# Layer 1's first attention turned round: P streamed past stationary features, denominators from a row of ones

## The chip, the core and the metric

The kernel runs on one core of one Trainium2 chip. The metric is the device time of one execution in microseconds, the median of several runs. Engines are named as in the profile: PE (matrix products), PEld (its weight loads), DVE (vector), ACT (activation), POOL, SP (issues the transfers).

## What is computed

Four graph-attention layers are applied to `x`, 32 batches of 512 nodes by 256 features, each after a layer norm and a relu. The change touches only the first of the two attentions in layer 1, where every node attends to every node (no mask), with 512 features:

```python
def _gat(inp, adj_mask, W, a):
    h = jnp.matmul(inp, W)
    f1 = jnp.matmul(h, a[:F_, 0])
    f2 = jnp.matmul(h, a[F_:, 0])
    e = jax.nn.leaky_relu(f1[:, :, None] + f2[:, None, :], ALPHA)
    ...
    att = jax.nn.softmax(e, axis=2)
    h_prime = jnp.einsum('bij,bjf->bif', att, h)
    return jax.nn.elu(h_prime)
out = jax.nn.relu(jnp.matmul(x, mlp1_w) + mlp1_b)
residual = out
out = _gat(jax.nn.relu(out), None, W_fc, a_fc)
out = jax.nn.elu(out) + residual
out = jax.nn.relu(jnp.matmul(out, mlp2_w) + mlp2_b)
```

Then comes a second attention under the mask, and layers 2 and 3. The elu is applied twice: for a negative y the result is exp(exp(y)-1)-1.

## The kernel before

Everything stays on the core. Batches run in three lanes (`s = b % 3`) with buffers of their own; each lane has a ring of PSUM banks, three for lanes 0 and 1, two for lane 2, and every use of a bank waits until its last reader is done (`freed`). Each engine has a generator per batch, cut into steps by `yield`; the strings in `TURNS` say, digit by digit, which batch's generator runs its next step on that engine. The order of every engine is thus fixed in the program, and in the steady state one cycle of it does one batch's worth of work, taken from up to six batches at once. Waits are on semaphores named for what is produced (`at("Plo", b, j)`).

Exact float32 products are made from three products of rounded parts (`mm3`, L516: hi by hi, hi by lo, lo by hi). ACT copies the high part out of a bank (`...hi`), DVE subtracts to get the low part (`...lo`).

In layer 1 of a batch: `turn` transposes the normalized input, `m1` is the first matrix, its relu stands in `O1` (features on the partitions, also the residual), its parts in `oT`. `project` (bank `h1`) gives features 256 to 511 and the scores, into `HA`; bank `hs2` gives features 0 to 255, into `HB`, which is the lane's `hT`. `HA` carries a column of ones. The exponentials P (source nodes on the partitions, 512 targets along the row) go to `R`, and their parts to `oT`, which is free by then (`Phi`, `Plo`). The attention itself is `attf`: for each block of 128 targets the block of P is the stationary operand and the features move past it, 258 columns of `HA` and 256 of `HB`; the ones give the denominator in column 256. So nodes lie on the partitions; ACT scales by the reciprocal (L1145, L1147) and the elu is done on 256 columns at a time by ACT and DVE (L878, L884, L1136). Since `m2` wants features on the partitions, 16 transposes (`zT`, L658) turn the result, and DVE adds it to `O1` (L902). `top` (L552) and `row` (L562) spread a maximum and a row of scores over the partitions, `attend` (L574) and the loop at L607 are the other attentions, `weigh` (L779) makes their P.

Of the kernel before, what the change touches and what calls it, by code (L numbers as in the profile page):

```python
# [34 lines left out]
    "Phi": (4,), "Plo": (4,), "attf": (8,), "rDf": (4,),  # L35
# [16 lines left out]
    + [("attf", q, "ef", (q, 1)) for q in range(8)] + [("zT", k, "o2", (k,)) for k in range(4)]  # L52
# [29 lines left out]
    "dve": (
        ("wwwwwwwww0000ww0000000000000ww000w000w0000w00ww0w0w0w000001w10000w00110w1110000101011100100000000010"
         "111000000w000101000100001100100000000111111000111111010100000010001000000022000101110212002112112210"
         "2202120010201211201121101120100001020111111221211212010110112111111111211221200210112200002212122011"
         "110000000"),
        ("2122222221122202022111212201100001110221000020120012202211110211211222112201210201101010111111112211"
         "12111111111101000022201110022220010100211122122222"),
        ("5455555555445535345454545534355344334343453535453545444454435453445345545435443534434443433443554544"
         "3444443344443444435355444335553534343535344455455545443444444342444343243344233234432232223424223443"  # L90
         "4423333324333332422434422442343343323332233223334324433333233333332342434332244242422332442334334443"
         "4433333223331332123323323322112332221131131231332132222113222223233123132313221213121222221113222322"
         "3122222222222211113313222131331311212311322223333233221222221222201210212122100122111120000201002211"
         "2211021121111202120200012201112000011111011211102211110110100210111111202101120200220012102221111211"
         "0011111111110111020101001102002011011011000001001010111010100010000000000111000000001000001001001111"
         "000000001000000000000001000001100000100000100000000000001010000000"),
    ),
# [66 lines left out]
def build(nc, x_d, adj_d, L0_W, L0_a, m1_w, m1_b, m2_w, m2_b, fc_w, fc_a, ha_w, ha_a, L2_W, L2_a, L3_W, L3_a, out_d):  # L164
    ctx = ExitStack()
    with ctx:
# [571 lines left out]
        def vector_batch(e, w, b):  # L738
# [151 lines left out]
            for q in range(8):  # L890
# [4 lines left out]
                if q > 1:  # L895
                    yield from joined(q - 2)
# [433 lines left out]
```

## Time and profile before

| | us |
|---|---|
| median of three runs (3109.88 to 3122.49) | 3118.48 |
| time of the profiled execution | 3117.49 |
| its span, first to last instruction | 3115.7 |
| PE busy | 3039.2 |
| DVE busy | 2453.6 |
| ACT busy | 2326.1 |

The span is the time between the first and the last instruction in the trace; 1.8 us of the execution lie around it. Busy time counts each moment once for an engine. A PE busy time is no measure of what PE could do, since the end of each product is modelled and overlaps the next; the distance between two starts is the better price.

### The profile page before, as it was taken

The page shows a single profiled execution, that of the slowest core. Times are in us where ns is not written, and L with a number is a line of the kernel's source. Part 1 is how long each engine was busy: PE and PEld are TensorE (multiplying, and loading weights), DVE is VectorE, ACT ScalarE, POOL GpSimd, SP SyncE. Part 2 cuts the span into 40 slices and gives each one's busy share as a digit, 9 for nine tenths or more (in the row PEclk, how much of TensorE's full clock was granted, in tenths as well). Part 3 has the DMA queues.
Part 4 walks back from the last instruction along what each step waited for, and adds up shares of the span by engine and source line. Part 5 has one row for each costly group of instructions (what it writes and reads, how often), then busy time and mean ns, then how long its engine had stood idle before and what let it go on. Part 6 is the DMA issues. An engine that isn't in the chain of part 4 may idle for free.

```text
span 3115.7 us, 58739 instructions
## 1 busy us (share of the span) xinstructions
PE 3039.2 (98%) x21504; PEld 2843.7 (91%) x21504; DVE 2453.6 (79%) x7049; ACT 2326.1 (75%) x6303; POOL 202.2 (6%) x410
## 2 busy tenths in 40 slices
PE   7999999999999999999999999999999999999996
PEld 7899999999999999999999999999999999999985
DVE  5787887887887888877888878878878878878764
ACT  6678777777778777778777778777777787787674
POOL 2000000000000000000000000000000000000000
PEclk8999999999999999999999999999999999999997
DMA  2000000000000000000000000000000000000000
GB/s 75 1 8 15 15 15 15 15 1 15 15 15 15 15 1 15 15 15 15 15 1 15 15 15 15 8 7 15 15 15 15 2 14 15 15 15 8 1 8 14
DMA packets 16335, 41.54 MB, mean 13 GB/s; under 512 B 5296, under 2 KB 6832, under 8 KB 16048
## 3 DMA queue, kind: packets, MB, share of 16 engines
q1 hardware_dynamic: 16048, 37.77, 3.4%
q8 instruction: 173, 2.83, 0.4%
q14 instruction: 114, 0.93, 0.1%
HBM read 20.99 MB, written 16.78 MB: 12 GB/s over the span
## 4 chain that ended last, share of the span: by engine, by line
PE 85%; ACT 8%; DVE 6%; issue 1%; SPq 0%; POOL 0%; DMA 0%; DVEq 0%; POOLq 0%; ACTq 0%
PE bank L516 46%; PE bank L574 15%; PE bank L607 14%; ACT Z L1031 4%; PE bank L562 3%; PE bank L530 2%; PE bank L658 2%; DVE R L779 2%; PE bank L552 1%; DVE x L996 1%; DVE Z L993 1%; ACT Z L1183 1%; ACT Z L1189 1%; ACT Z L1178 0%; PE bank L684 0%
## 5 line engine op out<-in xcount | busy, mean ns | idle before, releaser
L574 PE MATMUL bank<-hw,R 128*128 128x257 f32 x3072 | 713.1, 385 | 4.0 <-ACT hw L1069 3.0
L574 PEld LDWEIGHTS bank<-hw,R 128*128 128x128 f32 x3072 | 572.9, 192 | 79.5 <-issue 4.6
L607 PEld LDWEIGHTS bank<-hw,R 128*128 128x128 f32 x4096 | 496.4, 193 | 8.3 <-issue 3.8
L607 PE MATMUL bank<-hw,R 128*128 128x65 f32 x4096 | 499.6, 271 | 3.6 <-DVE R L779 3.6
L779 DVE SCALAR_TENSOR_TENSOR R<-bank,E,mask_ne 128x512 f32<-128x512 f32 x640 | 450.3, 742 | 14.7 <-PE bank L562 12.9
L1031 ACT ACTIVATE Z<-x,nm,rs 128x256 f32<-128x256 f32 x512 | 283.4, 593 | 55.9 <-DVE x L996 34.1
L1234 POOL TENSOR_TENSOR rs<-ve,mhalf 128x4 f32<-128x4 f32 x128 | 134.6, 1052 | 2858.7 <-DVE ve L731 2141.3
L516 PE MATMUL bank<-wfc_hi,oThi 128*128 128x256 f32 (+1 forms) x1024 | 302.8, 296 | 1.9 <-DVE oTlo L858 1.9
L516 PE MATMUL bank<-wfc_lo,oThi 128*128 128x256 f32 (+1 forms) x1024 | 290.5, 284 | 0.0
L516 PE MATMUL bank<-wfc_hi,oTlo 128*128 128x256 f32 (+1 forms) x1024 | 290.5, 284 | 0.0
L1054 ACT COPY Z<-bank 128x258 f32<-128x258 f32 (+1 forms) x512 | 183.5, 370 | 100.9 <-PE bank L516 100.4
L516 PEld LDWEIGHTS bank<-wfc_hi,oThi 128*128 128x128 f32 x1024 | 194.7, 190 | 3.7 <-DVE oTlo L858 2.6
L516 PEld LDWEIGHTS bank<-wfc_hi,oTlo 128*128 128x128 f32 x1024 | 195.2, 191 | 0.0
L516 PEld LDWEIGHTS bank<-wfc_lo,oThi 128*128 128x128 f32 x1024 | 195.0, 190 | 0.1
L1069 ACT ACTIVATE hw<-Z,hw 128x256 f32<-128x256 f32 x384 | 180.0, 502 | 1.2
L562 PE MATMUL bank<-identr,E 128*128 128x128 f32 x1024 | 154.2, 275 | 8.2 <-ACT E L1063 8.2
L516 PE MATMUL bank<-HAhi,oThi 128*128 128x258 f32 x512 | 161.0, 314 | 0.3 <-DVE oTlo L872 0.3
L1145 ACT ACTIVATE Z<-bank,rD 128x256 f32<-128x256 f32 x256 | 123.1, 481 | 45.2 <-DVE rD L893 37.9
L530 PE MATMUL bank<-identr,Z 128*128 128x128 f32 x1024 | 139.8, 280 | 10.3 <-ACT Z L1031 10.0
L516 PE MATMUL bank<-HAlo,oThi 128*128 128x258 f32 x512 | 145.4, 284 | 0.0
L516 PE MATMUL bank<-HAhi,oTlo 128*128 128x258 f32 x512 | 145.1, 283 | 0.0
L1008 ACT ACTIVATE Z<-x,sx 128x256 f32<-128x256 f32 x256 | 128.5, 505 | 20.2 <-DVE x L970 20.1
(260 smaller groups left out, 8306.1 us busy)
## 6 DMA issues: line engine op xcount, KB each, us to landing
x<-in_x_dram SPq DMA_DIRECT2D x32, 512.0 KB, 3.4
out_dram<-x SPq DMA_DIRECT2D x32, 512.0 KB, 2.6
R<-in_adj_dram SPq DMA_DIRECT2D x2, 512.0 KB, 5.9
Z<-in_L_gnn_mlp_w_dram SPq DMA_DIRECT2D x2, 512.0 KB, 5.4
O<-in_L_gnn_W_fc_dram SPq DMA_DIRECT2D x1, 1024.0 KB, 6.9
R<-in_L_gnn_W_dram SPq DMA_DIRECT2D x1, 256.0 KB, 3.7
R<-in_L_gnn_W_hand_dram SPq DMA_DIRECT2D x1, 256.0 KB, 6.7
rowt<-in_L_gnn_W_dram SPq DMA_DIRECT2D x1, 256.0 KB, 4.7
```

The costliest lines, as they stand in the source:

```text
L516: i = e.matmul(out, u, v, start=first and q == 0, stop=last and q == 2, skip_group_check=not group)
L530: i = e.transpose(bk[:, n * 128:(n + 1) * 128], hn[:, n, k * 128:(k + 1) * 128], ident[:, :])
L562: i = e.transpose(bk[:, n * 128:(n + 1) * 128], m["E"][:, 0, h, n:n + 1].broadcast_to([128, 128]), ident[:, :])
L574: ins = e.matmul(bk[:, 0:257], P[:, j, i * 128:(i + 1) * 128], hw[:, j, 0:257], start=(j == 0), stop=(j == NBLK - 1))
L607: ins = e.matmul(bk[:, i * 66:i * 66 + 65], P[:, (4 * h + j) % PTILES, i * 128:(i + 1) * 128], hv[:, j, h, 0:65], start=(j == 0 and i == 0 ...
L779: e.scalar_tensor_tensor(P[:, t, :], bank_of(b, "row", p)[:, :], m["E"][:, 1, h, j:j + 1], mask[:, j, :], ALU.max, ALU.mult).then_inc(up(" ...
L1008: e.activation(hns[b % LANES][:, n, :] if l else junk[:, n, :], xs[b % XSLOTS][:, n, :], ACT.Square, bias=m["sx"][:, n:n + 1], scale=-floa ...
L1031: e.activation(hn[:, n, :], x[:, n, :], ACT.Relu, bias=m["nm"][:, n:n + 1], scale=m["rs"][:, n:n + 1]).then_inc(up("hn", b))
L1054: e.copy(raw[s][:, i, 0:n], bank_of(b, f"h{l}", i)[:, 0:n]).then_inc(up("raw", b))
L1069: e.activation(hw[:, n, 0:256], raw[s][:, n, 0:256], ACT.Copy, scale=hw[:, n, 256:257]).then_inc(up("hw", b))
L1145: e.activation(Z[s][:, q * 256:(q + 1) * 256], bank_of(b, "attf", q)[:, 0:256], ACT.Relu, scale=rd).then_inc(up("ef", b))
L1234: e.tensor_tensor(m["rs"][:, :], m["ve"][:, :], mhalf[:, :], ALU.pow).then_inc(up("rs", b))
```

## The change

The roles in `attf` are exchanged. 128 features of `HA` or `HB` are now stationary (`FO` is the order of the four blocks), and the 512 columns of P move past them, so results have features on the partitions, 512 nodes along the row. The denominators come from eight products of their own (`dn`) with a stationary block of ones, which put them on all partitions of one bank. DVE takes the reciprocal of that bank, 512 wide, multiplies each result by it, adds the positive part to `O1` and cuts the negative part (`value`); ACT does two exponentials, DVE the last addition (`joined`). The transposes and their additions are gone. The parts of the sum are kept in `HA` and `hT` instead of `oT`. `m2` takes its blocks in the order of `FO`. `TURNS` is written anew for all engines.

```diff
 ONCE = {
...
-    "Phi": (4,), "Plo": (4,), "attf": (8,), "rDf": (4,),
-    "ef": (8, 2), "mf": (8,), "ef2": (8,), "zf": (8,), "zT": (4,), "o2": (4,), "o2hi": (4,), "o2lo": (4,),
+    "Phi": (4,), "Plo": (4,), "dn": (1,), "rDf": (1,), "attf": (4,), "yf": (4, 3), "ef": (4, 2), "o2": (4,),
+    "o2hi": (4,), "o2lo": (4,),
...
-    + [("attf", q, "ef", (q, 1)) for q in range(8)] + [("zT", k, "o2", (k,)) for k in range(4)]
+    + [("dn", 0, "rDf", (0,))] + [("attf", t, "yf", (t, 0)) for t in range(4)]
...
 TURNS = {
     "pe": (
-        ("wwww00w00000w000000w000ww0ww00ww000ww0w0w0w001www1w1w100w0000110100010000100121111000000000000100111"
+        ("wwwww00ww0000w0000000ww0000011w0w00000ww0001w11w1ww1w00w11000011000w01101000w001111w0w01000010011w100"
...
-        HA = {p: sb(f"HA{p}", [128, NBLK, F + 2], F32R) for p in PARTS2}
+        HA = {p: sb(f"HA{p}", [128, NBLK, F], F32R) for p in PARTS2}
+        FO = (2, 3, 0, 1)
+        ones = sb("ones", [128, 2], F32R)
+        HA2 = {p: HA[p].rearrange("p (k h) n -> p k (h n)", h=2) for p in PARTS2}
+        hwf = [hws[s].rearrange("p b n -> p (b n)") for s in range(LANES)]
+        rden = [hwf[s][:, 512:1024] for s in range(LANES)]
+        yfb = [[R[s][:, 4, :], rowt[s][:, :], hwf[s][:, 0:512]] for s in range(LANES)]
...
-            for q in range(8):
-                i, H, n = q // 2, (HA, HB[s])[q % 2], 258 - q % 2 * 2
-                cols = slice(i * 128, (i + 1) * 128)
-                w.wait_ge(*freed(b, "attf", q))
+            w.wait_ge(*freed(b, "dn", 0))
+            w.wait_ge(s_id, 1)
+            for j in range(NBLK):
+                w.wait_ge(*at("Plo", b, j))
+                for p in PARTS2:
+                    i = e.matmul(bank_of(b, "dn", 0)[:, :], ones[:, 0:1].broadcast_to([128, 128]), oT[p][:, j, :],
+                                 start=j == 0 and p == "hi", stop=j == NBLK - 1 and p == "lo")
...
+            for t, fo in enumerate(FO):
+                H, c0 = (HB[s], HA)[fo // 2], fo % 2 * 128
+                w.wait_ge(*freed(b, "attf", t))
                 for j in range(NBLK):
-                    w.wait_ge(*at("Plo", b, j))
-                    w.wait_ge(*at(("hAlo", "hBlo")[q % 2], b, j))
-                    ins = mm3(e, bank_of(b, "attf", q)[:, 0:n], (oT["hi"][:, j, cols], oT["lo"][:, j, cols]),
-                              (H["hi"][:, j, 0:n], H["lo"][:, j, 0:n]), j == 0, j == NBLK - 1)
...
+                    w.wait_ge(*at(("hBlo", "hAlo")[fo // 2], b, j))
+                    ins = mm3(e, bank_of(b, "attf", t)[:, :], (H["hi"][:, j, c0:c0 + 128], H["lo"][:, j, c0:c0 + 128]),
+                              (oT["hi"][:, j, :], oT["lo"][:, j, :]), j == 0, j == NBLK - 1)
...
-            for fo in range(4):
-                w.wait_ge(*freed(b, "zT", fo))
...
-                    i = e.transpose(bk[:, n * 128:(n + 1) * 128], Z[s][:, n * 512 + c0:n * 512 + c0 + 128], ident[:, :])
...
+                            tuple((HA2, hT[s])[t // 2][p][:, t % 2, :] for p in PARTS2), t == 0, t == 3)
...
+            def value(t, fo):
+                y = yfb[s][t % 3]
+                w.wait_ge(*at("attf", b, t))
+                e.tensor_tensor(y, bank_of(b, "attf", t)[:, :], rden[s], ALU.mult).then_inc(up("yf", b))
+                w.wait_ge(*at("yf", b, t, 0))
+                e.scalar_tensor_tensor(O1[:, fo, :], y, 0.0, O1[:, fo, :], ALU.max, ALU.add).then_inc(up("yf", b))
+                e.tensor_scalar(y, y, 0.0, None, ALU.min).then_inc(up("yf", b))
+                yield
+
+            def joined(t, fo):
+                w.wait_ge(*at("ef", b, t, 1))
+                w.wait_ge(*at("yf", b, t, 1))
+                e.scalar_tensor_tensor(O1[:, fo, :], yfb[s][t % 3], -1.0, O1[:, fo, :], ALU.add, ALU.add).then_inc(up("o2", b))
+                yield
...
+            w.wait_ge(*at("dn", b, 0))
+            e.reciprocal(rden[s], bank_of(b, "dn", 0)[:, :]).then_inc(up("rDf", b))
...
+            for t, fo in enumerate(FO):
+                yield from value(t, fo)
+                if t > 0:
+                    yield from joined(t - 1, FO[t - 1])
+                if t > 1:
+                    yield from low_o2(t - 2, FO[t - 2])
...
-                w.wait_ge(*at("m2", b - 1, 1))
+                w.wait_ge(*at("attf", b - 1, 3))
                 w.wait_ge(*at("o2lo", b - 1, 3))
...
+            for t in range(4):
+                y = yfb[s][t % 3]
+                w.wait_ge(*at("yf", b, t, 2))
+                e.activation(y, y, ACT.Exp).then_inc(up("ef", b))
+                yield
+                w.wait_ge(*at("ef", b, t, 0))
+                e.activation(y, y, ACT.Exp, bias=minus1[:, 0:1]).then_inc(up("ef", b))
```

What moves on the engines is shown at three places of the steady state. Names are those of the buffers: `hw2,R2` is the attention of lane 2, `tm0` the maximum of lane 0, `Z` holds normalized input or projected features. First PE after the projection of layer 1's second attention (`wha`), before the change:

```order
L516 MATMUL bank0<-wha_hi,hT0lo 128x258
L574 MATMUL bank7<-hw2,R2 128x257 [waits P_2,hw_2,sc_2]
L552 MATMUL bank1<-identr,tm0 128x128 [waits sc_0,raw_0]
L574 MATMUL bank7<-hw2,R2 128x257 [waits P_2,hw_2] x3
L562 MATMUL bank2<-identr,E0 128x128 [waits E_0,raw_0]
L562 MATMUL bank2<-identr,E0 128x128 x3
L574 MATMUL bank6<-hw2,R2 128x257 x4
L574 MATMUL bank7<-hw2,R2 128x257 [waits y3_2]
```

PE at the same place with the change:

```order
L520 MATMUL bank2<-wha_hi,hT0lo 128x258
L578 MATMUL bank6<-hw2,R2 128x257 [waits P_2,hw_2] x3
L556 MATMUL bank0<-identr,tm0 128x128 [waits sc_0,raw_0]
L578 MATMUL bank7<-hw2,R2 128x257 x4
L566 MATMUL bank1<-identr,E0 128x128 [waits E_0,raw_0]
L566 MATMUL bank1<-identr,E0 128x128 x3
L578 MATMUL bank6<-hw2,R2 128x257 [waits y3_2]
L578 MATMUL bank6<-hw2,R2 128x257 x3
```

Three products of lane 2 instead of one stand ahead of the transpose of `tm0`.

Second PE between the transposes for `m1` and `m1` itself, before the change:

```order
L530 MATMUL bank3<-identr,Z1 128x128 [waits hn_1] x4
L530 MATMUL bank4<-identr,Z1 128x128 [waits y0]
L530 MATMUL bank4<-identr,Z1 128x128 x3
L530 MATMUL bank7<-identr,Z2 128x128 [waits hn_2,y3_2]
L530 MATMUL bank7<-identr,Z2 128x128 [waits hn_2] x3
L530 MATMUL bank6<-identr,Z2 128x128 [waits y3_2]
L530 MATMUL bank6<-identr,Z2 128x128 x3
L516 MATMUL bank5<-hT1hi,wm1_hi 128x512 [waits hTlo_1,y0]
L516 MATMUL bank5<-hT1lo,wm1_hi 128x512
```

PE at the same place with the change:

```order
L534 MATMUL bank3<-identr,Z1 128x128 [waits hn_1] x4
L534 MATMUL bank4<-identr,Z1 128x128 [waits y0]
L534 MATMUL bank4<-identr,Z1 128x128 x3
L520 MATMUL bank6<-w0_hi,hT2hi 128x264 [waits raw_2]
L520 MATMUL bank6<-w0_lo,hT2hi 128x264
L520 MATMUL bank6<-w0_hi,hT2lo 128x264
L520 MATMUL bank6<-w0_hi,hT2hi 128x264
L520 MATMUL bank6<-w0_lo,hT2hi 128x264
L520 MATMUL bank6<-w0_hi,hT2lo 128x264
L520 MATMUL bank7<-w0_hi,hT2hi 128x264 [waits raw_2]
L520 MATMUL bank7<-w0_lo,hT2hi 128x264
L520 MATMUL bank7<-w0_hi,hT2lo 128x264
```

The transposes of lane 2 stood between; now four steps of `w0` products do, of which the last three rows are not shown; after them comes `m1`.

Third DVE. Before the change, from the first `attf` of a batch on:

```order
L893 RECIPROCAL rD0<-bank1 128x1 [waits attf]
L968 SCALAR_TENSOR_TENSOR Z2<-Z2 128x256 [waits e2]
L970 SCALAR_TENSOR_TENSOR x0,sx2<-Z2,x0 128x256 [waits x2]
L878 TENSOR_SCALAR R0<-R0 128x256 [waits ef]
L779 SCALAR_TENSOR_TENSOR R1<-bank4,E1,mask_ne 128x512 [waits row_1]
L731 TENSOR_SCALAR ve2<-sq2 128x4 [waits sq_2]
L779 SCALAR_TENSOR_TENSOR R1<-bank4,E1,mask_ne 128x512 [waits att0]
L878 TENSOR_SCALAR R0<-R0 128x256 [waits ef]
L893 RECIPROCAL rD0<-bank0 128x1 [waits attf]
L779 SCALAR_TENSOR_TENSOR R1<-bank4,E1,mask_ne 128x512 [waits att0]
L884 SCALAR_TENSOR_TENSOR Z0<-R0,Z0 128x256 [waits ef2]
L779 SCALAR_TENSOR_TENSOR R1<-bank4,E1,mask_ne 128x512 [waits att0]
```

The products that wait on these rows are `attf` of lane 0. DVE with the change, from the variance of lane 2 (`ve2`) on:

```order
L732 TENSOR_SCALAR ve2<-sq2 128x4 [waits sq_2]
L899 RECIPROCAL hw0<-bank1 128x512 [waits dn]
L780 SCALAR_TENSOR_TENSOR R1<-bank4,E1,mask_ne 128x512 [waits att0,rDf]
L780 SCALAR_TENSOR_TENSOR R1<-bank4,E1,mask_ne 128x512 [waits att0]
L879 TENSOR_TENSOR R0<-bank2,hw0 128x512 [waits attf]
L881 SCALAR_TENSOR_TENSOR O1<-R0,O1 128x512 [waits yf]
L882 TENSOR_SCALAR R0<-R0 128x512
L780 SCALAR_TENSOR_TENSOR R1<-bank4,E1,mask_ne 128x512 [waits att0]
L879 TENSOR_TENSOR rowt0<-bank0,hw0 128x512 [waits attf]
L881 SCALAR_TENSOR_TENSOR O1<-rowt0,O1 128x512 [waits yf]
L882 TENSOR_SCALAR rowt0<-rowt0 128x512
```

The next rows of DVE there:

```order
L888 SCALAR_TENSOR_TENSOR O1<-R0,O1 128x512 [waits ef]
L879 TENSOR_TENSOR hw0<-bank1,hw0 128x512 [waits attf]
L881 SCALAR_TENSOR_TENSOR O1<-hw0,O1 128x512 [waits yf]
L882 TENSOR_SCALAR hw0<-hw0 128x512
L747 TENSOR_TENSOR hT2lo<-bank7,hT2hi 128x512 [waits hThi_2]
L747 TENSOR_TENSOR hT2lo<-bank6,hT2hi 128x512 [waits hThi_2]
L793 CAST hsr2<-hs2 128x2
L795 TENSOR_TENSOR hsr2<-hs2,hsr2 128x2 [waits hs_2]
```

The reciprocal of 512 columns stands behind the variance `ve2` and ahead of two blocks of P of lane 1 (`R1`), and the low parts `hT2lo` and the sums `hsr2` of lane 2 stand behind three whole `value` steps.

## Rows read from the trace of the kernel before

**Rows 1.** The page: its head and section 1.

```profile
span 3115.7 us, 58739 instructions
...
PE 3039.2 (98%) x21504; PEld 2843.7 (91%) x21504; DVE 2453.6 (79%) x7049; ACT 2326.1 (75%) x6303; POOL 202.2 (6%) x410
```

**Rows 2.** Windows, 400 to 2800: busy us (count) of PE, PEld, DVE, ACT, POOL; clock.

```profile
400.00:2800.00 2400.00, 2379.73 (x17008) 2231.24 (x17007) 1936.72 (x5594) 1838.33 (x5003) 149.46 (x309) 1.00 0.04 13
```

**Rows 3.** Chain of waits in order of time: start, us, what.

```profile
1520.90 0.87 PE bank L658 x8
...
1531.20 0.84 PE bank L607 x8
...
1536.98 2.73 DVE R L779 x4
...
1543.48 5.22 PE bank L574 x24
...
1630.82 2.73 DVE R L779 x4
```

**Rows 4.** Timeline of PE, 1514 to 1531: start, us, instruction.

```profile
1515.67 0.28 PE L516 MATMUL bank<-hT0hi,oThi 128*128 128x256 f32 x1
...
1517.09 0.60 PE L562 MATMUL bank<-identr,E 128*128 128x128 f32 x4
...
1525.79 0.40 PE L516 MATMUL bank<-oTlo,wm_hi 128*128 128x512 f32 x1
...
1530.81 0.39 PE L516 MATMUL bank<-oThi,wm_lo 128*128 128x512 f32 x1
```

**Rows 5.** Groups by form, DVE and ACT: busy us, mean ns of one, idle before.

```profile
L902 DVE TENSOR_TENSOR O<-bank,O 128x512 f32<-128x512 f32 x128 | 85.3, 686 | 59.0 <-PE bank L658 59.0
...
L867 DVE TENSOR_SCALAR R<-rowt,E 128x512 f32<-128x512 f32 x128 | 63.4, 536 | 0.0
...
L884 DVE SCALAR_TENSOR_TENSOR Z<-rowt,Z 128x256 f32<-128x256 f32 x128 | 54.1, 424 | 13.9 <-ACT rowt L1136 6.8
...
L878 DVE TENSOR_SCALAR R<-R 128x256 f32<-128x256 f32 x128 | 37.3, 293 | 40.9 <-ACT R L1147 40.9
...
L1145 ACT ACTIVATE Z<-bank,rD 128x256 f32<-128x256 f32 x256 | 123.1, 481 | 45.2 <-DVE rD L893 37.9 <-PE bank L516 3.0 <-issue 0.6
...
L1136 ACT ACTIVATE R<-R,minus 128x256 f32<-128x256 f32 x128 | 67.1, 524 | 0.2 <-DVE R L878 0.2
...
L1147 ACT ACTIVATE rowt<-bank,rD 128x256 f32<-128x256 f32 x128 | 63.0, 492 | 0.0
...
L1090 ACT ACTIVATE Z<-Z 128x256 f32<-128x256 f32 x128 | 53.4, 417 | 4.1
```

**Rows 6.** The three lines with RECIPROCAL: ns min/median/max of one.

```profile
L788 DVE RECIPROCAL rD<-D x384: 162/164/166, 138.0 to 3110.7; 128x1 f32<-128x1 f32 x192
...
L834 DVE RECIPROCAL rD<-D x128: 177/178/180, 34.7 to 2947.6; 128x4 f32<-128x4 f32 x128
...
L893 DVE RECIPROCAL rD<-bank x128: 154/168/170, 97.2 to 3015.6; 128x1 f32<-128x1 f32 x128
```

**Rows 7.** Timeline at 1555 to 1558, PE and DVE, ahead of `m1`.

```profile
1555.46 2.02 PE L530 MATMUL bank<-identr,Z 128*128 128x128 f32 x16
1557.92 0.47 PE L516 MATMUL bank<-hT1hi,wm_hi 128*128 128x512 f32 x1 [0.44 <-DVE hT1lo L746]
...
1557.09 1.29 DVE L746 TENSOR_TENSOR hT1lo<-bank,hT1hi 128x512 fp32r<-128x512 f32 x2 [0.25 <-ACT hT1hi L1048]
```

**Rows 8.** Timeline of PE at 1540 to 1542, ahead of layer 1's maximum.

```profile
1540.44 0.60 PE L574 MATMUL bank<-hw,R 128*128 128x257 f32 x2
1541.36 0.29 PE L552 MATMUL bank<-identr,tm 128*128 128x128 f32 x1 [0.33 <-DVE tm L753]
```

**Rows 9.** Timeline, 1502 to 1507: end of layer 2's attention, then its variance.

```profile
1502.29 0.47 PE L516 MATMUL bank<-HAhi,oThi 128*128 128x258 f32 x1
...
1506.81 0.17 DVE L731 TENSOR_SCALAR ve<-sq 128x4 f32<-128x4 f32 x1
```

More of the change, by code:

```diff
@@ L885, in joined @@
                 yield
-            def exf(q):
-                return (R[s][:, 4, 0:256], R[s][:, 4, 256:512], rowt[s][:, 0:256], rowt[s][:, 256:512])[q % 4]
-            for q in range(8):
-                if q % 2 == 0:
-                    w.wait_ge(*at("attf", b, q))
-                    e.reciprocal(m["rD"][:, 0, q // 2:q // 2 + 1], bank_of(b, "attf", q)[:, 256:257]).then_inc(up("rDf", b))
-                    yield
-                if q > 1:
-                    yield from joined(q - 2)
-                yield from small(q)
@@ L898, in vector_batch @@
-            yield from joined(6)
-            yield from joined(7)
-            for k in range(4):
-                w.wait_ge(*at("zT", b, k))
-                e.tensor_tensor(O1[:, k, :], bank_of(b, "zT", k)[:, :], O1[:, k, :], ALU.add).then_inc(up("o2", b))
-                yield
-                if k:
-                    w.wait_ge(*at("o2hi", b, k - 1))
-                    e.tensor_tensor(oT["lo"][:, k - 1, :], O1[:, k - 1, :], f32(oT["hi"][:, k - 1, :]),
-                                    ALU.subtract).then_inc(up("o2lo", b))
-                    yield
@@ L1129, in scalar_batch, with parts @@
                 yield
[L1131 to L1154 removed]
+            def parts(t):
+                w.wait_ge(*at("o2", b, t))
+                w.wait_ge(*at("attf", b, t // 2 * 2 + 1))
+                e.copy((HA2, hT[s])[t // 2]["hi"][:, t % 2, :], O1[:, FO[t], :]).then_inc(up("o2hi", b))
+                yield
+            for t in range(4):
+                y = yfb[s][t % 3]
+                w.wait_ge(*at("yf", b, t, 2))
+                e.activation(y, y, ACT.Exp).then_inc(up("ef", b))
+                yield
+                w.wait_ge(*at("ef", b, t, 0))
+                e.activation(y, y, ACT.Exp, bias=minus1[:, 0:1]).then_inc(up("ef", b))
                 yield
+                if t:
+                    yield from parts(t - 1)
+            yield from parts(3)
             for fo in range(2):
@@ L1284, in _ @@
             w.wait_ge(s_const, 1)
-            for p, q, v in (("hi", F, -2.0), ("hi", F + 1, 0.0), ("lo", F, 0.0), ("lo", F + 1, 0.0)):
-                e.tensor_scalar(HA[p][:, :, q], mhalf[:, :], v, None, ALU.mult)
+            e.tensor_scalar(ones[:, :], mhalf[:, 0:2], -2.0, None, ALU.mult)
             e.tensor_copy(identr[:, :], id_st).then_inc(s_id)
```

140 lines of the change are left out of this document (56 added, 84 removed).

## The prediction

> **What bounds the kernel now.** I read the page's busy times first. PE is busy for 98% of the span, DVE for 79%, ACT for 75% [rows 1]. In the steady stretch PE is busy for 2379.7 of 2400 us at full clock, DVE for 1936.7, 81% [rows 2]. So the end of every batch's work is set by PE, and another engine costs something only where PE waits for it. The chain of waits in order of time gives the length of a cycle: the same piece, four blocks of P by L779, comes at 1536.98 and again at 1630.82, 93.84 us later [rows 3]. Some 28 of the 32 batches pass in this manner; the rest is ramp and tail.
>
> PE's busy time is modelled, so I price its products by the distance of starts. Twelve products of 256 columns take from 1515.67 to 1517.09, 0.118 each; 22 steps of 512 columns take from 1525.79 to 1530.81, 0.228 each [rows 4]. A transpose is 0.87/8 = 0.109, a 65-column product 0.84/8 = 0.105 (0.21 for one in the program, which issues two), a 257-column one 5.22/24 = 0.2175 (0.435 in the program) [rows 3].
>
> Where does PE wait in the cycle? Two places. Ahead of `m1`, 16 transposes begin at 1555.46 and are issued by 1555.46 + 16 x 0.109 = 1557.20, but the first product starts at 1557.92, after DVE's low part began at 1557.09: 0.7 us lost [rows 7]. Ahead of `tm0`, two halves of a 257-column product from 1540.44 end at 1540.88, the transpose starts at 1541.36: 0.5 us lost [rows 8]. With small waits behind both I take 1.5 us of old waits in a cycle.
>
> **PE's own work.** Removed per batch: 96 products of 256 or 258 columns, 96 x 0.118 = 11.33, and 16 transposes, 1.74, together 13.07 us. Added: 8 + 48 = 56 products of 512 columns, 56 x 0.228 = 12.77. Saved: 0.30 a batch, 10 us in all. The columns are nearly equal; what is saved is half the starts. Unknown is whether the products with a broadcast block of ones cost the same: between 0.118 (the cheaper product, -0.9 a batch) and 0.24 I take 0.228, since the engine streams the same 512 columns.
>
> **The old waits.** The new order puts three 257-column products of lane 2 ahead of `tm0` where one stood: 2 x 0.435 = 0.87 more cover against 0.5 lost [rows 3, 8]. Between the second half of the transposes and `m1` stand twelve `w0` products, 12 x 0.118 = 1.4, where eight transposes stood, 0.87: 0.55 more against 0.7 lost [rows 3, 4, 7]. Both waits go nearly or wholly: -1.5.
>
> **ACT.** Removed: 8 relus (L1145, 0.481), 8 exponentials (L1147, 0.49), 8 with a bias (L1136, 0.52): 11.9 us [rows 5]. Added: four of each exponential at 512 columns. No exponential of 512 columns is in the rows; the 256 more cost between nothing and DVE's step for as many, 0.686 - 0.42 = 0.27, and I take 0.21, nearer to the latter since the engine streams too: 0.417 + 0.21 = 0.63 (L1090) and 0.73, together 5.5. ACT loses 6.4 us a batch. It is not the bound, so this is worth nothing by itself.
>
> **DVE.** Removed: 8 x 0.29 (L878), 8 x 0.42 (L884), 4 x 0.686 (L902), 4 x 0.168 (L893): 9.1 us [rows 5, 6]. Added four times: the multiplication from the bank 0.69 (as L902), the positive part 0.69, the cut 0.54 (as L867), the joining 0.69: 10.4 us, 1.95 of it in one `value` step. Then one reciprocal of 512 columns, which no row shows. Bounds: if it streamed like L902, 0.69. By L788 and L834, one column takes 164 ns and four take 178, so 4.7 ns a column: 164 + 511 x 4.7 = 2.55 us. By the farthest pair (154 of L893, 180 of L834), 8.7 ns a column: 4.6 us [rows 6]. I take 2.55, because the medians are of the same operand and spread by 2 ns. DVE's load then rises from 1936.7/2400 x 93.84 = 75.7 us a cycle [rows 2, 3] by 3.9 to 79.6 of some 92: it is still not the bound, but its order becomes tight.
>
> The page "VectorE: DVE Perf Modes" of the Trainium skill, section "First, the fixed hardware budget", says that the reciprocal is an iterative divide with a repeat count of 8. If that meant eight cycles a column at the 0.96 GHz it gives, one would take about 4.4 us (an estimate from the page), and the sum below would be 1.9 us a cycle higher. The step of 4.7 ns in the rows is nearer to half of that.
>
> **The new wait.** It is in DVE's order after `dn`. Put zero where PE has issued the last `dn`. PE's list from there: two `attf` of 12 x 0.228 = 2.74 (done 5.5), 1.3 us of lane 1, the third `attf` (6.8 to 9.5), eight transposes of lane 2, the fourth (10.4 to 13.2), then the small products `hsr2`, which need DVE's `hT2lo` and `hsr2`. DVE: `ve2` closes layer 2's norm. Before, the next product after that attention starts at 1502.29 and `ve` at 1506.81, 4.5 us [rows 9]; part of this is DVE's other work, so I take 3.6, and the attention now ends 1.8 before zero. The reciprocal behind `ve2` thus runs from 1.8 to 4.35; two blocks of P at 2.73/4 = 0.68 [rows 3] to 5.7; `value` to 7.7; P to 8.4; `value` to 10.3; the joining to 11.0; `value` to 13.0; two `hT2lo` (0.69) to 14.4; `hsr2` to about 14.8. PE wants it at 13.2: a new wait of 1.6 us. Behind it are queued, on PE, lane 2's last projection and `m2` of lane 0, so the whole cycle moves. Going on likewise, the third low part of the sum, behind three more joinings and a `value`, reaches `m2` some 0.4 to 0.5 late; I take 0.2 more for other places with less cover than before. New waits: 2.3, none of which I can see in a row; the bounds are 0.3 (a short reciprocal, the third `value` then waits only for its product) and 4.3 (the long one).
>
> **Sum.** Per cycle -0.30 - 1.5 + 2.3 = +0.5, and over 28 cycles +14, less the saving on the four other batches, 1: from the profiled 3117.5 to about 3130. The old waits' remainder could be larger than 1.5 and my walk ignores that DVE catches up; I put the median 5 us lower, 3125. The profiled execution is within 1 us of the median of the runs, so no shift is needed.
>
> **Rivals.**
> Fast: the reciprocal takes about 1 us or less, or DVE reaches it earlier. Then the wait ahead of `hsr2` is at most 0.3 and `m2`'s is gone; -0.30 - 1.5 + 0.5 = -1.3, 28 times: 3080, at best 3065. For it: all three old waits lose their cause and bank rings are used five times instead of twelve. Against: the 4.7 ns step.
>
> Slow: the reciprocal takes 3.5 to 4.6 us. It stands on the DVE path to `hsr2`, so each us above 2.55 is a us of PE, from the point where DVE is already late (about 1 us, by the walk). 0.95 to 2.05 more, 28 times: 3157 to 3187. For it: the farthest pair of rows. Against: the medians. The rule of that page of the Trainium skill would give about 4.4 us and so 3170, by the same walk.
>
> No effect: 512-column products at 0.236 and no reciprocal wait but the old ones elsewhere: 3118. It falls into the same band as my forecast.
>
> DVE as the bound: at 79.6 + 2 it would need 10 us more a cycle; I give it nothing of its own.
>
> **Chances.** The forecast (reciprocal near 2.6, waits exchanged, 3100 to 3150) 0.45; fast 0.30; slow 0.25. A difference of about 0.5%, 15.6 us, is what a measurement of this kernel can tell from none. Of the first case I put 0.34 within it, 0.04 below, 0.07 above; of the fast case nearly all is below, of the slow one nearly all above. Faster 0.33, same 0.36, slower 0.31. The range takes in the fast case from 3065 and the slow one to 3175; the forecast's own range is 3100 to 3150.
>
> **What the profile will show.** Right: PE's products of 512 columns 0.23 apart and 19,700 instructions instead of 21,504; RECIPROCAL 128x512 near 2.6 us; no idle ahead of `tm0` and `m1`; PE idle ahead of the first product on `hsr`, put down to DVE; DVE at about 85% in the steady stretch, ACT at 70%. Wrong: the reciprocal off by over 1 us either way; or PE waiting ahead of something that I did not list, such as layer 1's projection behind the last `m1`, or the transposes of layer 0.

## The result, and the profile after

The changed kernel takes 3189.5 us (median of 4 runs, 3185.6 to 3193.7) against 3114.2 us (3109.7 to 3122.5) for the kernel before on the same chip: ratio 1.024, 95% interval 1.021 to 1.027. The forecast was 3125, its range ended at 3175. The time is lost in the steady part. I take the length of a cycle from the start of the four transposes ahead of layer 0's maximum in one batch to the same in the next, mean over 22 cycles: 94.10 us before, 96.66 after, and 28 x 2.56 = 72 of the 75 us. Executions of one and the same kernel fall into two groups 8 to 16 us apart, with a higher and a lower mean granted clock (0.991 and 0.985 in the kernel before), so small differences are read from the cycle and not from the medians.

The page after, its head and busy times:

```profile
span 3183.8 us, 54320 instructions
...
PE 3065.3 (96%) x19712; PEld 2750.1 (86%) x19712; DVE 2607.4 (82%) x6822; ACT 2195.4 (69%) x5791; POOL 206.0 (6%) x410
```

The window from 400 to 2800 us of the same trace, columns as in [rows 2]:

```profile
400.00:2800.00 2400.00, 2341.25 (x15198) 2103.57 (x15197) 2006.07 (x5271) 1690.60 (x4479) 145.63 (x297) 1.00 0.03 12
```

PE lost 38 us of busy time in the window, DVE gained 69, ACT lost 148. The mean clock rounds to 1.00, as in [rows 2], but it is not full throughout. In the kernel before no stretch of this window is at the lower of the two levels; here four are, 3.4 us each, at 778, 1358, 1938 and 2518 us. One of them by the same view, and two products of 512 columns in it on PE's timeline, which start 0.43 us apart:

```profile
1357.85:1361.27 3.42, 3.40 (x10) 2.90 (x11) 2.29 (x4) 2.06 (x4) 0.00 (x0) 0.51 0.00 0
...
1359.63 0.63 PE L520 MATMUL bank<-oThi,hT1lo 128*128 128x512 f32 x1
1360.06 0.63 PE L520 MATMUL bank<-oThi,hT1hi 128*128 128x512 f32 x1
```

At full clock they are 0.23 apart. Each of the four stretches begins within 0.3 us of the end of a wait of 1.85 us, and the cycle that holds it lasts 98.3 us where the cycle at the same place of the three lanes' rotation lasts 96.8: 1.5 us more. So 6 of the 72 us are the clock's.

The groups of instructions, by form, give the prices that no row showed before:

```profile
L899 DVE RECIPROCAL hw<-bank 128x512 f32<-128x512 f32 x32 | 107.2, 3351 | 0.0
...
L881 DVE SCALAR_TENSOR_TENSOR O<-R,O 128x512 f32<-128x512 f32 x64 | 44.3, 692 | 2.2
...
L879 DVE TENSOR_TENSOR R<-bank,hw 128x512 f32<-128x512 f32 x64 | 43.7, 683 | 0.1
L882 DVE TENSOR_SCALAR R<-R 128x512 f32<-128x512 f32 x64 | 26.9, 420 | 0.0
```

The two exponentials on ACT, in the same view:

```profile
L1144 ACT ACTIVATE R<-R,minus 128x512 f32<-128x512 f32 x64 | 45.8, 715 | 0.9
L1141 ACT ACTIVATE R<-R 128x512 f32<-128x512 f32 x64 | 40.5, 633 | 127.4 <-DVE R L882 127.3
```

The reciprocal takes 3.35 us, not 2.55. The waits of PE over the whole execution (engine, what waited, for whom: us in all, times, the longest):

```profile
PE bank L534 <- ACT Z L1030: 16.8, 23, 8.4
PE bank L520 <- DVE hw L899: 16.4, 11, 1.7
PE bank L520 <- DVE oTlo L859: 16.0, 26, 0.6
PE bank L566 <- DVE R L780: 14.8, 8, 1.9
PE bank L520 <- DVE hsr L795: 9.2, 10, 1.9
```

The first line is ramp and tail: 0.9 of its 16.8 us fall between 400 and 2800 us. The old waits ahead of `m1` and `tm0` [rows 7, 8] are gone from this list. Four others stand in it: for the reciprocal itself, for the last low part ahead of layer 1's projection (L859), for a block of P that stood behind the reciprocal (L780), and the one that I had forecast, for `hsr`. The forecast wait, on PE's timeline at 1558 us:

```profile
1557.68 0.40 PE L520 MATMUL bank<-oThi,hT0lo 128*128 128x512 f32 x1
1558.96 0.38 PE L520 MATMUL bank<-w_hi,hsr 128*128 128x256 f32 x1 [0.88 <-DVE hsr L795]
```

DVE's timeline of the same stretch, from the reciprocal to what PE waits for:

```profile
1545.84 3.35 DVE L899 RECIPROCAL hw<-bank 128x512 f32<-128x512 f32 x1
...
1557.36 1.28 DVE L747 TENSOR_TENSOR hT2lo<-bank,hT2hi 128x512 fp32r<-128x512 f32 x2
...
1558.75 0.16 DVE L795 TENSOR_TENSOR hsr<-hs,hsr 128x2 fp32r<-128x2 f32 x1
```

One cycle earlier, on PE's timeline between the first and the second `attf`, a wait that I had not forecast:

```profile
1450.45 0.40 PE L520 MATMUL bank<-oThi,HAlo 128*128 128x512 f32 x1
1452.57 0.50 PE L520 MATMUL bank<-oThi,HAhi 128*128 128x512 f32 x1 [1.72 <-DVE hw L899]
```

And one cycle later, on PE's timeline, the other one, ahead of a row of transposes:

```profile
1648.84 0.54 PE L566 MATMUL bank<-identr,E 128*128 128x128 f32 x3 [1.85 <-DVE R L780]
```

The same wait three cycles earlier ends at 1357.87. DVE's timeline ahead of it:

```profile
1350.70 3.35 DVE L899 RECIPROCAL hw<-bank 128x512 f32<-128x512 f32 x1
1354.09 1.41 DVE L780 SCALAR_TENSOR_TENSOR R<-bank,E,mask_ne 128x512 f32<-128x512 f32 x2
1355.41 0.68 DVE L879 TENSOR_TENSOR R<-bank,hw 128x512 f32<-128x512 f32 x1
...
1357.07 0.75 DVE L780 SCALAR_TENSOR_TENSOR R<-bank,E,mask_ne 128x512 f32<-128x512 f32 x1
```

The transposes need a bank that is free when the fourth and last block of P has read it (`freed`). That block stands behind the reciprocal and the first `value` step; the two right behind the reciprocal are the second and the third, and nothing of PE waits for them here.

The wait at 1452.57 is one for a bank. Lane 2 has two banks; the first `attf` sits in one, `dn` in the other, and the second `attf` needs the bank that the reciprocal still reads (`rDf` frees it). Lanes 0 and 1 have three.

### The profile page after: what moved, and what is told of

It is laid out like the page before. It is cut to its first block, busy times and chain, and to the rows that moved or that the text cites. A ratio compares the mean times of both kernels' runs of the same rounds, so it can differ in the third digit from the quotient of the medians.

```text
span 3183.8 us, 54320 instructions
## 1 busy us (share of the span) xinstructions
PE 3065.3 (96%) x19712; PEld 2750.1 (86%) x19712; DVE 2607.4 (82%) x6822; ACT 2195.4 (69%) x5791; POOL 206.0 (6%) x410
## 4 chain that ended last, share of the span: by engine, by line
PE 62%; DVE 20%; ACT 16%; issue 1%; POOL 0%; SPq 0%; DMA 0%; POOLq 0%; DVEq 0%; ACTq 0%
PE bank L520 32%; PE bank L611 12%; PE bank L578 11%; DVE R L780 5%; ACT Z L1030 4%; DVE hw L899 3%; PE bank L566 2%; ACT oThi L1105 2%; ACT O L1103 2%; PE bank L534 2%; DVE Z L992 1%; DVE x L995 1%; ACT Z L1171 1%; PE bank L685 1%; ACT Z L1176 1%
## 5 line engine op out<-in xcount | busy, mean ns | idle before, releaser
L578 PE MATMUL bank<-hw,R 128*128 128x257 f32 x3072 | 725.9, 384 | 3.6 <-ACT hw L1068 1.0
L780 DVE SCALAR_TENSOR_TENSOR R<-bank,E,mask_ne 128x512 f32<-128x512 f32 x640 | 458.4, 744 | 30.2 <-PE bank L611 23.8
L534 PE MATMUL bank<-identr,Z 128*128 128x128 f32 x1024 | 146.2, 280 | 18.7 <-ACT Z L1030 16.8
L566 PEld LDWEIGHTS bank<-identr,E 128*128 128x128 f32 x1024 | 119.6, 143 | 42.5 <-issue 21.6
L534 PEld LDWEIGHTS bank<-identr,Z 128*128 128x128 f32 x1024 | 120.2, 143 | 37.2 <-ACT Z L1030 18.4
L1218 ACT ACTIVATE Z<-bank,rD 128x256 f32<-128x256 f32 x128 | 59.3, 465 | 131.7 <-DVE rD L789 131.5
L1141 ACT ACTIVATE R<-R 128x512 f32<-128x512 f32 x64 | 40.5, 633 | 127.4 <-DVE R L882 127.3
```

The costliest lines, as they stand in the source:

```text
L534: i = e.transpose(bk[:, n * 128:(n + 1) * 128], hn[:, n, k * 128:(k + 1) * 128], ident[:, :])
L566: i = e.transpose(bk[:, n * 128:(n + 1) * 128], m["E"][:, 0, h, n:n + 1].broadcast_to([128, 128]), ident[:, :])
L578: ins = e.matmul(bk[:, 0:257], P[:, j, i * 128:(i + 1) * 128], hw[:, j, 0:257], start=(j == 0), stop=(j == NBLK - 1))
L780: e.scalar_tensor_tensor(P[:, t, :], bank_of(b, "row", p)[:, :], m["E"][:, 1, h, j:j + 1], mask[:, j, :], ALU.max, ALU.mult).then_inc(up(" ...
```

## Experiments on the reciprocal

Theory A: the loss is the time that DVE spends on the reciprocal. The rivals were that the new order or the new waits cost by themselves. The first four kernels:

```diff
# e1_no_reciprocal, in the changed kernel (the quotient is a constant, the division is left out)
-            e.reciprocal(rden[s], bank_of(b, "dn", 0)[:, :]).then_inc(up("rDf", b))
+            e.tensor_scalar(rden[s], bank_of(b, "dn", 0)[:, :], 0.0, 2e-29, ALU.mult, ALU.add).then_inc(up("rDf", b))
# e2_reciprocal_twice: a second one, unused, into yfb[s][2]
# e3_half_reciprocal: 256 columns divided, the other 256 set to a constant (half the division left out)
# e4_before_with_reciprocal, in the kernel before, ahead of the first small reciprocal; its result is unused
+                        e.reciprocal(R[s][:, 4, :], P[:, 0, :])
```

> The kernel after with the 512-wide reciprocal replaced by one tensor_scalar of the same bank (times 0 plus a constant), about 0.65 us in place of 3.35; the division by the denominators is left out, all else stays. Theory A, the length of the reciprocal on DVE is what PE waits for at three places (the second attf product and the row of lane 2, the sums of layer 3): 1.6 to 2.7 us a cycle come back, 3189 falls to 3115 to 3145, and the waits on L899, R L780 and hsr go. Rival B, the new order itself is bad (projection right behind m1, fewer covers), whatever DVE does: less than 15 us come back, 3175 or more.

Measured: 3125.5 us (ratio to before 1.001, 0.999 to 1.003), cycle 94.76 us.

> The kernel after with the reciprocal on 256 columns and a constant on the other 256 (half of the division left out): DVE 1.1 to 1.3 us shorter there. A: a line between the others, 25 to 35 us less than 3189, near 3155 to 3165. B: no change, 3185.

Measured: 3140.6 us (1.007, 1.005 to 1.010), cycle 95.23 us: 14 us below A's range, so half the columns give back three quarters of the loss. Its reciprocal of 256 columns took 1746 ns:

```profile
L900 DVE RECIPROCAL hw<-bank 128x256 f32<-128x256 f32 x32 | 55.9, 1746 | 0.0
```

> The kernel after with a second, unused 512-wide reciprocal of the same bank ahead of the one that counts: 3.35 us more of DVE at that place. A: DVE is already late there, so nearly all of it shows, 2.8 to 3.35 us a cycle, 3270 to 3290. B: DVE's time is not what PE waits for, under 3215.

Measured: 3333.9 us (1.070, 1.066 to 1.073), cycle 101.14 us: 4.5 us a cycle for the second 3.35 us, more than any theory had.

> The kernel before with one additional 512-wide reciprocal (of a tile of P, result unused) on DVE ahead of its first small one: 3.35 us more of DVE at the same place of the program. A: it costs there too, since DVE is 81% busy and its work is queued behind: 1 to 2.7 us a cycle, 3145 to 3190. B: the order before absorbs it, under 3130.

Measured: 3192.7 us (1.025, 1.022 to 1.029), cycle 96.66 us, 3 us above A's range. The reciprocal took 3345 ns, here on a tile in SBUF. That the cycle equals the changed kernel's is chance: in every third cycle of this trace the clock is at its lower level for 3.4 us, in the changed kernel in every sixth.

So the reciprocal's length accounts for 64 of the 75 us, and the kernel before, with none of the new order, loses as much to it. The cost is not linear: cycles of 94.76, 95.23, 96.66 and 101.14 us for 0.7 us (the step in its place), 2.2 (1.75 and a 0.42 us step for the other half), 3.35 and 6.64 us on DVE. The first 2 us are nearly covered.

The last step, 4.5 us of cycle for 3.3 us of DVE, has the clock in it. Over the same 22 cycles the granted clock is at its lower level for 105 us in e2, 10 in the changed kernel and 0 in e1 and e3; in e2 nearly all of it begins in waits of PE of 4.9 and 5.1 us, some 2 us before they end. The cycles of e2 without such a stretch last 99.0 us, against 95.8 at the same place of the rotation in the changed kernel: 3.2 more. The others are 5.4 to 5.6 longer and hold 6.8 us at half clock each, 4.6 to 5.2 of them behind the wait, which can cost 2.3 to 2.6 us (an estimate: half the work of that time). About 3 us are left. So what goes beyond the 3.3 us of DVE can be the clock's alone; no run here shows that DVE's time costs more than itself. Is it the time on DVE, and does it matter that it is in one piece?

```diff
# e5_reciprocal_on_act: on ACT, a step behind the squares; nothing stands for it on DVE; one table for both
+            e.activation(rden[s], bank_of(b, "dn", 0)[:, :], ACT.Ln, scale=2.0 ** -86).then_inc(up("lnd", b))
+            w.wait_ge(*at("lnd", b, 0))
+            e.activation(rden[s], rden[s], ACT.Exp, bias=lnc[:, 0:1], scale=-1.0).then_inc(up("rDf", b))
# e11_reciprocal_in_four: pieces 1 and 2 each followed by one step of the other lane's P, then pieces 3 and 4
+            for p in range(4):
+                cols = slice(p * 128, (p + 1) * 128)
+                e.reciprocal(rden[s][:, cols], bank_of(b, "dn", 0)[:, cols]).then_inc(up("rDf", b))
+                yield
```

> The changed kernel with the reciprocal of the denominators taken from DVE and computed on ACT instead, as exp(-ln(d)): two ACTIVATEs of 128x512 (0.63 and 0.72 us by the Exp rows of the changed kernel's trace), put on ACT behind the squares and ahead of the first normalising step, where ACT stands idle for 1.8 and 4.2 us. Nothing of the computation is left out. Theory A (the loss is the 3.35 us that DVE is held, once a batch): DVE is freed of it and the quotients are there sooner, so 3115 to 3130 us, as without the reciprocal (3125.5). Rival B (the loss comes from when the quotients are there, and from the new steps around them, whoever computes them): Ln and Exp end some 1.4 us behind the last product with ones instead of 3.4 us, so half of the loss at most comes back, 3150 to 3165. Rival C (ACT becomes late: 1.3 us more stand ahead of the normalising step and so of the transposes of layer 2's result): 3140 to 3160, with a new wait of PE for the normalised features.

Measured: 3127.5 us (1.001, 0.999 to 1.003), cycle 94.76 us, as without any reciprocal. A holds; B and C fall. On ACT the two take 0.58 and 0.73 us.

> The changed kernel with the reciprocal on DVE, cut into four of 128 columns (0.06 + 128 x 6.25 ns = 0.9 us each, 3.6 us in all), with the two steps of the other lane's P that stood behind it now behind the first and the second piece. Nothing is left out. Theory A1 (what costs is that DVE is occupied, whatever stands in between): 3186 to 3197 us. Theory A2 (what costs is that others' rows stand behind one piece of 3.35 us): these two come 2.5 and 1.7 us sooner, and a third to two thirds of the 64 us come back, 3145 to 3170.

Measured: 3221.2 us (1.030, 1.028 to 1.033), cycle 97.82 us: slower than in one piece, which neither A1 nor A2 gave. The source view of the line, with the shortest, median and longest ns of one:

```profile
L912 DVE RECIPROCAL hw<-bank x128: 893/948/953, 114.5 to 3121.6; 128x128 f32<-128x128 f32 x128
```

The two blocks of P came earlier, as meant, but PE's row waits for the fourth, behind the first `value` step. On DVE and PE:

```profile
1371.76 0.95 DVE L912 RECIPROCAL hw<-bank 128x128 f32<-128x128 f32 x1
...
1376.42 0.69 DVE L890 TENSOR_TENSOR R<-bank,hw 128x512 f32<-128x512 f32 x1
...
1378.09 0.75 DVE L791 SCALAR_TENSOR_TENSOR R<-bank,E,mask_ne 128x512 f32<-128x512 f32 x1
...
1378.89 0.65 PE L577 MATMUL bank<-identr,E 128*128 128x128 f32 x4 [1.81 <-DVE R L791]
```

From the start of the reciprocal to `value` are 4.66 us here and 4.71 in one piece, so this wait stays (1.81 for 1.85): A2 was tried on the two blocks that nobody waits for. The last piece ends 4.6 us behind the first's start instead of 3.35, and with it the bank of `dn` comes free later. Lane 2's second `attf` on PE's timeline:

```profile
1474.88 0.57 PE L531 MATMUL bank<-oThi,HAhi 128*128 128x512 f32 x1 [3.00 <-DVE hw L912]
```

The wait at this place is 3.00 us where it was 1.72: 1.3 us in one cycle of three. The rest is the clock. It is at its lower level for 3.4 us right behind this wait and behind the one for the row, in two cycles of three. The three cycles of the rotation last 99.7, 95.8 and 98.3 us, against 96.9, 95.8 and 96.8 in the changed kernel where the clock is full: 1.3 + 1.5, 0 and 1.5 us more.

## Experiments on the other 0.66 us

Without the reciprocal the cycle is still 94.76 against 94.10 us, though the old waits are gone. I added up, between 400 and 2800 us, every start of a product that comes more than 0.03 us later than the pace, which is the median distance of starts behind a product of the same form: 82.7 us before (3.2 a cycle), 105.3 in e5 (4.2), 151.6 in the changed kernel (6.1). What is left for PE's own work is 90.9, 90.6 and 90.6 us a cycle. Late starts behind an idle time that the profile records fell from 1.2 us a cycle before to 0.8 in e5; the many short ones, for which it records none, rose from 2.1 to 3.4, and I have not traced why. The largest place in e5 is layer 1's projection behind the last `m1`, 17.9 us. So the waits seemed to be the price, place by place. Theory W: cover one, and its time comes back.

```diff
# e6_h1_high_first (changed kernel), e7_both (the same on e5): PE, blocks 0 and 1 of layer 1's projection
-   per block and per k: hi x hi, hi x lo, lo x hi
+   both blocks, all k: hi x hi, hi x lo (wait for o1hi); then both blocks, all k: lo x hi (wait for o1lo)
# e8_before_m1_high_first (kernel before): the same within each m1 product, on hThi and hTlo
```

> The changed kernel, reciprocal on DVE as it was, with one order changed on PE: of the projection of layer 1, the products with the high part of the features come first, for two node blocks together, and those with the low part behind them, so that the last low part is wanted 12 products later. It covers the wait behind the last m1 product, 17.9 us in 23 between 400 and 2800 us of the changed kernel's trace (0.78 a cycle, some 0.85 with the small ones). If the two waits (this and the one for the late DVE) add up: 3189.5 - 0.8 x 32 = 3163, range 3157 to 3170. Rival: DVE's late stretch sets the cycle and takes up what is gained elsewhere, so 3180 to 3190, and the waits behind the reciprocal grow by what this one loses.

Measured: 3196.3 us (1.024, 1.020 to 1.027), above both ranges; cycle 96.65, unchanged.

> Both edits: reciprocal on ACT and high parts first in layer 1's projection. Theory A, with the waits adding up: 3125 - 0.8 x 32 = 3099, range 3090 to 3108, below the kernel before by 0.3 to 0.8%. Rival (what is freed is taken up by another wait, since PE runs against more chains than these): 3115 to 3125.

Measured: 3129.7 us (1.002, 1.000 to 1.004), above both ranges; cycle 94.66, 0.1 less than e5.

> The kernel before with one order changed on PE: in layer 1's first product (m1) the four products with the high part of the transposed features come first, the two with the low part behind them, so that the low part is wanted 4 products of 0.23 us later. The old wait there was put at 0.7 us a cycle in the prediction [rows 7]. If that wait was a real price: 3114 - 0.67 x 32 = 3093, range 3088 to 3100, and then the change's own gain from the old waits is real and was lost again elsewhere. Rival: DVE's chain behind it is as late, so the wait only moves to the next wait for DVE, and 3110 to 3118.

Measured: 3113.2 us (0.999, 0.996 to 1.001), cycle 94.10, unchanged.

Theory W falls three times. In e7 the wait for `oTlo` left the list of PE's waits, and the sum of late starts stayed, at 105.4 us. The chain of waits shows why. Its pieces off PE in one cycle of e5, in order of time:

```profile
1578.32 0.59 ACT Z L1017 x2
1578.91 0.58 ACT O L1113
1579.51 0.62 ACT oThi L1115
1580.13 0.60 ACT O L1113
1580.75 0.62 ACT oThi L1115
...
1582.39 0.57 ACT O L1113
1582.98 0.62 ACT oThi L1115
1583.60 0.60 ACT O L1113
1584.22 0.63 ACT oThi L1115
1584.88 0.70 DVE oTlo L871
```

and of e7, from the last of these on:

```profile
1581.74 0.60 ACT O L1129
1582.36 0.62 ACT oThi L1131
1582.98 1.50 ACT Z L1033 x6
1584.75 1.14 POOL rs L1259
1586.42 2.09 ACT Z L1056 x4
```

Here ACT works without a pause through the squares of one lane and the Relus and high parts of `m1` of another. With the projection's wait covered, PE meets the next product of the same ACT run, the normalised features of lane 2 (squares, POOL, L1056). The wait only changed its name. Theory D: this ACT run sets the cycle. Rival E: several chains are about as long.

```diff
# e12_extra_act_in_m1, on e5: one more ACT copy, unused, ahead of the last Relu of m1
+                if fo == 3:
+                    e.copy(junk[:, 0:2, :].rearrange("p a n -> p (a n)"), O1[:, 2, :])
# e9_m1_relu_on_dve, on e5, and e10_relu_and_h1, on e7: m1's bias and Relu on DVE in 22 of 32 batches
-                e.activation(O1[:, fo, :], bank_of(b, "m1", fo)[:, :], ACT.Relu, bias=b1[:, fo:fo + 1])
+                e.tensor_scalar(O1[:, fo, :], bank_of(b, "m1", fo)[:, :], b1[:, fo:fo + 1], 0.0, ALU.add, ALU.max)
# e13_less_act_in_m1, on e5; e14_less_act_and_h1, on e7; e15_before_less_act_in_m1, on the kernel before:
# the Relu writes oT["hi"], the copy from O1 is left out (residual not written, low part zero)
```

> The kernel with the reciprocal on ACT and one more, unused, ACT copy of 128x512 (0.6 us) ahead of the last Relu of the first product of layer 1. It adds work whose result nobody reads. If the run of ACT work there is on the chain that sets the cycle (D, and E too, since with several chains any one that grows takes over): 3127 + 0.6 x 32 = 3146, range 3140 to 3150. If it only looks so in the chain view and PE's wait there is covered elsewhere: 3125 to 3132.

Measured: 3141.2 us (1.005, 1.003 to 1.007), within the range, cycle 95.28: 0.52 us more for a copy that now stands in the chain with 0.52 us (0.61 by its own duration):

```profile
1576.16 0.52 ACT junk L1114
1576.68 0.60 ACT O L1115
```

> The kernel with the reciprocal on ACT (3127.5 us, cycle 94.76 us), and with the bias and Relu of the first product of layer 1 (four ACTIVATEs of 128x512, 0.6 us each) moved from ACT to DVE (tensor_scalar from PSUM, 0.69 us by the nearest rows) in 22 of the 32 batches; the other ten keep them on ACT. Nothing is left out. In the chain that ended last, that kernel's cycle goes through an unbroken run of ACT work at this place, 6.5 us of squares, Relus and high parts from 1578.3 to 1584.9. Theory D (this run of ACT work is what sets the cycle once the reciprocal is gone): up to 2.4 us leave it, the next chain takes over, cycles of 94.76 become 94.0 to 94.3, 3127 less 10 to 17 us = 3110 to 3117. Rival E (PE runs against several chains of the same length, as the covered layer-1 projection already suggests): 3122 to 3130.

Measured: 3195.5 us (1.023, 1.021 to 1.025), cycle 97.67: both theories missed. 22 batches lost 68 us, 3.1 each, where DVE got 4 x 0.745 = 3.0. Part of it is the clock again, at its lower level for 27 us in the 22 cycles; the cycles without such a stretch last 97.4 us, 2.6 more than in e5. DVE has no room at this place either; the chain goes through its steps instead of ACT's.

> The run before with the high parts first in layer 1's projection as well. Theory D: the wait for the low part and the late normalising of the other lane are both eased, cycle below 94.1 (that of the kernel before), 3095 to 3112 us. Rival E: again no more than 0.1 us a cycle, 3118 to 3130.

Measured: 3187.4 us (1.019, 1.016 to 1.022), cycle 97.22: missed likewise.

> The kernel with the reciprocal on ACT (3127.5 us, cycle 94.76 us), with the four separate copies that make the high parts of layer 1's first product left out: the Relu writes the high part directly, the residual stays unwritten, and the low part becomes zero. So four ACT instructions of 0.6 us each are gone a batch, and DVE and PE do what they did. If the run of ACT work there alone sets the cycle (D): 94.76 falls to 93.9 or less, 3127 less 27 us or more, 3080 to 3102. If other chains are about as long (E): a gain of 0.1 to 0.4 us a cycle, 3113 to 3125.

Measured: 3110.6 us (0.996, 0.994 to 0.998), 17 us less than e5 for 4 x 0.6 = 2.4 us of ACT work in each of 31 batches. The time lies between D's range and E's. The profiled execution was a single one of 11,779 us, in which products of 512 columns start 0.84 us apart, so its trace says nothing of the others and there is no cycle to give.

> The same, with the high parts first in layer 1's projection as well. D: the same as the run before it or some us less, 3075 to 3100. E: if the normalising of the other lane is the next chain, the earlier end of the projection gives nothing by itself, 3110 to 3125.

Measured: 3117.6 us (0.999, 0.997 to 1.001), in E's range; cycle 94.20, 0.46 less than e7.

> The kernel before, with the same four copies left out in the same way. Its chain of waits does not pass this run of ACT work but the transposes and the low part ahead of the first product. D: no more than 0.1 us a cycle, 3112 to 3122 us. E: both kernels gain alike, 0.1 to 0.4 us a cycle, 3105 to 3115.

Measured: 3106.4 us (0.998, 0.996 to 1.001), in E's range; cycle 93.95.

The ACT run is on the chain (e12 pays in full), but 2.4 us less of it give back only some 0.5 us a cycle, and 0.15 in the kernel before. That is nearer to E than to D: several chains of nearly the same length would give it, though they were not laid open one by one. What holds the 0.66 us stays open, as does the quarter of a microsecond between e14 and e15 (94.20 against 93.95), where both leave out the same ACT work. In the whole time the 0.66 us shows as 5 to 8 us and not 18, since the tail behind the last batch's mark is 7 to 12 us shorter (215 to 216 us in e1, e5 and e7, 228 before and 222 in e8). No version that computes the whole result beats the kernel before by more than the measurement can tell; e13, at 0.996, leaves part of it out.

## Why the prediction was wrong

Two steps failed: the price of the reciprocal (22 us) and the credit for the old waits (42 us); from the sum's 3130 the miss is 60 us. The cost of a long reciprocal, once its price is known, came near.

**The price of the reciprocal**: "I take 2.55, because the medians are of the same operand and spread by 2 ns". It measured 3.351, and 0.8 x 28 = 22 us of the miss are this. The rows for one and four columns [rows 6] are 14 ns apart, and I stretched that slope by a factor of 170. The measured widths are 128, 256 and 512 columns at 948, 1746 and 3351 ns: 6.26 ns a column between the first and the last. With the 0.96 GHz that the page "VectorE: DVE Perf Modes" of the Trainium skill gives in "Specifications", that is six cycles a column. The page's repeat count of 8, read as eight cycles a column, gave about 4.4 us; the trace disagrees with that reading as it does with my slope. My bounds, 0.69 to 4.6, held the value. The 3170 that the slow rival gives for 4.4 us is a slip: 3130 + 1.9 x 28 is 3183.

**The old waits**, -1.5 us a cycle or 42 us: they went, as forecast, but the time did not come back. The fast rival, this kernel with a reciprocal of 1 us or less, was put at 3080; e1 is that case and measured 3125.5, e5 3127.5, with a cycle of 94.76 where that rival has 93.84 - 1.3 = 92.5. e8 covered the wait ahead of `m1` in the kernel before, and its cycle stayed at 94.10 us. A wait of PE in a row is where a chain that runs through other engines happens to meet PE; if that chain is what sets the cycle, covering the meeting point moves it on. That this is so here is what e8, e6 and e7 suggest; the chain itself was not shown for the kernel before.

**The slow rival** was near in mechanism: beyond what is covered, a microsecond of the reciprocal is about one of PE. Its band, 3157 to 3187, reaches to within 3 us of the result, but for 3.5 us and more of reciprocal and on a base that was too low; at 3.35 my walk gives 3130 + 0.8 x 28 = 3152. From the fast rival's 3080 that would be a cost of 72 us, and 64 were measured, some of them through the clock.

**The new waits** were put at 2.3 us a cycle by one walk along DVE to `hsr2`, for all lanes alike. The three waits behind the reciprocal come to 38.5 us in the window, 1.6 a cycle, so the size was within the bounds, but the places were not those of the walk. That wait came small: 7.3 us in the window, 0.3 a cycle, and `m2`'s did not come. The walk looked only forward to the value steps. It passed over who else stands behind the reciprocal: the last block of the next lane's P, and with it PE's next row (16.1 us, 0.65 a cycle), and the bank of `dn`, which lane 2 needs at once (15.1 us, 0.6). Both follow from the rings of banks and from DVE's list alone. With 17.9 us (0.7) ahead of layer 1's projection, which I had named only as a sign of being wrong and which is there without the reciprocal too (17.9 in e5), they make 56 of the 152 us of late starts.

**The clock** is not in the prediction at all: 1.5 us for each stretch of 3.4 us at the lower level, 6 us in the changed kernel.

**PE's own work**, -0.30 us: 90.9 before, 90.6 after, by the sums above. Priced alone, the exchanged products save less. In the two traces the medians are 0.118 for 256 columns, 0.121 for 258 and 0.233 to 0.234 for 512, not 0.228 as in [rows 4]: 13.2 us go and 13.1 come. Those with the block of ones cost the same 0.23. **ACT**: exponentials of 0.63 and 0.72 us against 0.63 and 0.73. **DVE**: 0.69 and 0.68 as forecast, the cut 0.42 instead of 0.54; its load is 2006.07/2400 x 96.66 = 80.8 us a cycle against 79.6. These loads were forecast well. The conclusion that DVE costs "nothing of its own" was drawn from its share of the cycle and does not hold: in e9, with DVE 82% busy, 3.0 us more of it made the cycle 2.9 us longer, 2.6 where the clock is full.

## What to carry to other kernels

A slope from rows of one and four columns says little about 512; measure such a form alone when the change stands or falls with it. When a long step is put into the list of an engine that serves several lanes, ask three things and not one: who waits for its result, who stands behind it in the list, and which buffer it holds until it ends. And in a schedule tightened over all its engines a wait in a row is no price: before counting a gain from covering it, follow the chain of waits a whole cycle and see whether it leaves the engine there. Last, a mean clock of 1.00 can hide stretches at half clock: when a cycle costs more than the work put into it, look at the granted clock behind the longest waits.

## Not expected of the hardware

RECIPROCAL on DVE took 3351 ns for 128x512 from PSUM and 3345 in SBUF (e4), where a TENSOR_TENSOR of that shape took 683 to 692 ns: five times as long. The same quotient as exp(-ln(d)) on ACT took 0.58 + 0.73 = 1.3 us. A TENSOR_SCALAR of 128x512 with two operations, reading PSUM, took 683 ns with two constants (e1) and 745 with a bias of one value per partition (e9); a plain minimum in SBUF took 420. PE's granted clock fell to half for 3.4 us at the end of every second wait of 1.85 us in the changed kernel and of each of 2.18 us in e4 and 3.00 in e11, and for 6.8 us, beginning inside the wait, with those of 4.9 and 5.1 us in e2.
